# Last attention step and tail of the FFN in another order: probability copy before the maxima, gate chunks before the other batches' steps, down products before z, and z in two banks

## The chip, the cores and the metric

One Trainium2 chip, one core of it. The time is the device time in microseconds of one execution; the median of three runs is compared. Engines are named PE (TensorE), DVE (VectorE), ACT (ScalarE), POOL (GpSimd) and SP (SyncE, which issues the loads).

## The reference

Four layers over x of 8 batches x 128 tokens x 512, each added to its input after a layer norm without weights:

```python
x = x + cross_attention(layernorm(x), ctx, mask, bias, ...)   # 32 heads of 128, softmax over 128 keys
x = x + ffn(layernorm(x), w_gate, w_up, w_down)               # int8 fake quantisation, silu(gate) * up, 1376 wide
x = x + channel_attention(layernorm(x), ctx, conv_w, ...)     # top 76 of 128 of ctx per column, max/mean, conv, batch norm
x = x + routed_lora(layernorm(x), router_w, A, Bm)            # 8 experts, best 2
```

The third layer splits z = layernorm(x), transposed, by a mask of the context's largest values into two parts, takes the maximum and the mean of each over the tokens, sends both through a small convolution, and normalises over all batches: every batch's maxima and sums must be there before the convolution can start.

## The kernel before, in words

Each engine has one instruction stream, written out by hand; semaphores (`s_...`) are the only order between the engines, and an engine that waits holds all that stands behind it. Batches 0 to 3 go through 32 attention steps (one per head) first, then batches 4 to 7 through steps 32 to 63, in which the FFN and the z part of batches 0 to 3 are hidden (`turn(n, r)`). What is left behind step 63 is the tail: batches 4 to 7 (called k = 0 to 3 there) go through the FFN and the z part with nothing to hide them.

In step 63 PE makes scores in `pS`, DVE adds bias and mask, takes maxima, ACT takes exponentials, DVE multiplies by the inverse row sums (`prob`), PE transposes `prob` into `pS`, DVE copies it to `pT_sb` (L1402), PE makes `pT` from it and the values (L1983), ACT and DVE split that into `aT_hi` and `aT_lo` (L1351), and PE adds the output projection to `oacc` (L1731 to L1733, four batches, `outputs`). DVE also looks for the largest context values in every step (`pick_round`, MAX8 and MATCH_REPLACE, L1194 to L1200), and writes the found mask to `top` (L1413) in each fourth. `e_zshift` (L1396) is a shift for ACT's `z_again`.

In the tail, in this order for each k: `residual_of(k)` (L1454) adds `oacc` to `xr`; `token_stats` and POOL's `token_rstd` give the norm; `token_steps` (L1471 to L1480) the quantised tokens; PE transposes them, ACT writes `t_yqT` (`tokens_out`); PE's `gate_products` and `up_products` (L2043) fill `pA` in three chunks of 512, 512 and 352 columns; DVE's `gate_rows(k, j)` (L1489) empties a gate chunk, and only then PE may write the up chunk of the same columns; ACT's `gated_silu` and `up_out` and POOL's `up_rows` follow; `hidden(k)` (DVE, L1496 to L1506) multiplies and quantises; `hidden_transposes`, ACT's `hidden_out` (L976), `down_products` (PE into `pD`, L2078), `down_rows` (DVE, L1514); then `xr` takes the sum (`add_down` on POOL, or DVE in `z_stats`). For z: `z_stats(k)`, POOL's `z_rstd(k)`, DVE's `z_shift(k)` and ACT's `z_normal(k)` (or `z_here(k)`, all on DVE), PE's `z_transposes(k)`, then the split into `split` (ACT `z_out` and POOL `branches`, or DVE `branches_here`), DVE's `maxima(k)` (L1448) and ACT's `sums(k)` (L935). `pTb`, `pA`, `pD`, `pZ`, `pYb` are PSUM tensors that lie where the attention's `oacc`, `pX0`, `pX1`, `pS` and `pT` were; `s_x1_done` guards that. `z_transposes` had one bank, `pZ`.

Of the kernel before, what the change touches and what calls it, by code (L numbers as in the profile page):

```python
# [52 lines left out]
def layers_kernel(nc, x, cT, mask, bias, ln_w, wq, wk, wv, wo, w_gate, w_up, w_down,  # L53
# [12 lines left out]
    with ctx:  # L66
# [1033 lines left out]
        def _(dve):  # L1100
# [251 lines left out]

            def step(n, half, q, j, rows=False):
# [37 lines left out]
                if isinstance(n, int) and n == STEPS - 1:  # L1391
                    dve.wait_ge(s_e_zrs, HB)
                    dve.wait_ge(s_e_z_trans, HB - 1)
                    v.tensor_scalar(e_down[:], xr[:, HB - 1, :], e_zmv[:, HB - 1, 0:1], e_zrs[:, HB - 1:HB],
                                    ALU.subtract, ALU.mult).then_inc(s_e_z_t, 1)
                    v.scalar_tensor_tensor(out=e_zshift[:], in0=e_zmv[:, :, 0], scalar=-1.0, in1=e_zrs[:],  # L1396
                                           op0=ALU.mult, op1=ALU.mult).then_inc(s_e_zshift, 1)
# [7 lines left out]
                if j < 3:  # L1405
                    pick_round()
                else:
                    dve.drain()
                    for r in range(2):
                        tile = bass.ds(half * KT * NH + (2 * q + r) * S, S)  # L1410
                        if isinstance(q, int):
                            tile = slice(half * KT * NH + (2 * q + r) * S, half * KT * NH + (2 * q + r + 1) * S)
                        v.tensor_scalar(top_flat[:, tile], pick[:, r, ::-1], LOWEST, None, ALU.not_equal)  # L1413
# [311 lines left out]
        def _(pe):  # L1725
# [356 lines left out]
            def z_transposes(k):  # L2082
                if k < 2:
                    pe.wait_ge(s_z_act, k + 1)
                else:
                    pe.wait_ge(s_z_dve, k - 1)
                if k in (1, 2):
                    pe.wait_ge(s_zT, k)
                if k == 3:
                    pe.wait_ge(s_split_dve, 2)  # L2090
# [178 lines left out]
```

## Time and profile before

| | us |
|---|---|
| three runs | 1065.75, 1065.99, 1067.38 |
| median | 1065.99 |
| the profiled execution, its own time | 1069.71 |
| its span in the trace | 1068.0 |
| end of the last attention step's output products, start of the convolution | 946.4, 1013.6 |

The span runs from the first to the last instruction. The profiled execution's own time is 1.7 us above its span and 3.7 us above the median of the runs. All that the change touches lies between 933 us and 1014 us of the span.

### The profile page before, as it was taken

Reading aid. Unit: us, or ns where it says so; the run is one execution under the profiler, and the core shown is the slowest. Engines: PE = TensorE matmul, PEld = TensorE weight load, DVE = VectorE, ACT = ScalarE, POOL = GpSimd, SP = SyncE. Lnnn points to the kernel's source line nnn. Section 1 sums busy time; section 2 is a strip of 40 time slices with the busy share of each in tenths; the row PEclk is TensorE's granted clock in tenths of the full one; section 3 lists DMA queues with packets and bytes.
Section 4 is the critical chain, followed back from the end, with each engine's and each line's share of the span. In section 5 each row is a group of like instructions: output and inputs, shape, how many; then the busy total and the mean of one; then the engine's idle time right before and its main releaser. Section 6 shows DMA issues by size and latency. Waiting matters only on the chain.

```text
span 1068.0 us, 18238 instructions
## 1 busy us (share of the span) xinstructions
PE 996.8 (93%) x6004; PEld 843.0 (79%) x6004; DVE 697.6 (65%) x1827; ACT 512.6 (48%) x1328; POOL 467.5 (44%) x366
## 2 busy tenths in 40 slices
PE   5999999999999999999999999999999999869376
PEld 4888888888888888888888888888888888734263
DVE  5567565666577767677564575566567557678755
ACT  4454444444444445445543544445355354345561
POOL 4555444444444555443354344346435334226241
PEclk9999999999999999999999999999999999969768
DMA  6422222223333332333322222213222221000002
GB/s 219 161 92 87 95 95 89 91 95 96 96 97 98 98 97 83 104 112 98 106 84 84 85 67 72 83 42 98 73 74 84 80 69 53 23 21 1 0 2 79
DMA packets 50412, 87.71 MB, mean 82 GB/s; under 512 B 6368, under 2 KB 15200, under 8 KB 50336
## 3 DMA queue, kind: packets, MB, share of 16 engines
q1 hardware_dynamic: 50336, 86.76, 25.4%
q8 instruction: 40, 0.66, 0.2%
q14 instruction: 36, 0.29, 0.1%
HBM read 84.64 MB, written 2.10 MB: 81 GB/s over the span
## 4 chain that ended last, share of the span: by engine, by line
PE 79%; DVE 7%; issue 6%; POOL 3%; DVEq 2%; ACT 2%; DMA 1%; SPq 0%; POOLq 0%; ACTq 0%
PE pX L1731 15%; PE pX L1733 14%; PE pX L1732 14%; PE pT L1983 5%; PE oacc L1731 5%; PE oacc L1732 5%; PE oacc L1733 5%; PE pS L1915 5%; PE pS L1736 2%; PE pA L2043 1%; POOL wv_lo L570 1%; PE pX L1848 1%; PE pX L1904 1%; PE pT L1904 1%; PE pX L1736 1%
## 5 line engine op out<-in xcount | busy, mean ns | idle before, releaser
L570 POOL TENSOR_TENSOR wq_lo<-raw_q,wq_hi 128x512 fp32r<-128x512 f32 x64 | 82.6, 1290 | 264.2 <-DVE prob L1376 257.9
L1731 PE MATMUL pX<-wv_lo,cT_hi 128*128 128x256 f32 x512 | 149.5, 292 | 0.2 <-ACT q_sb L740 0.2
L1359 DVE TENSOR_TENSOR score<-pS,b_mask 128x512 f32<-128x512 f32 x64 | 44.2, 691 | 156.8 <-PE pS L1915 144.7
L868 ACT ACTIVATE prob<-score,neg_max 128x128 f32<-128x128 f32 x256 | 99.8, 391 | 97.4 <-DVE neg_max L1362 97.4
L1732 PE MATMUL pX<-wv_hi,cT_lo 128*128 128x256 f32 x512 | 144.3, 282 | 0.0
L1733 PE MATMUL pX<-wv_hi,cT_hi 128*128 128x256 f32 x512 | 144.2, 282 | 0.0
L570 POOL TENSOR_TENSOR wv_lo<-raw_v,wv_hi 128x1024 fp32r<-128x1024 f32 x32 | 77.1, 2409 | 121.9 <-ACT wv_hi L740 121.9
L740 ACT ACTIVATE v_sb<-pX 128x512 f32<-128x512 f32 x64 | 38.2, 597 | 163.6 <-PE pX L1733 163.6
L1731 PE MATMUL pX<-xT_lo,wq_hi 128*128 128x512 f32 x252 | 104.4, 414 | 5.7 <-POOL wq_lo L570 5.0
L1731 PE MATMUL oacc<-wo_lo,aT_hi 128*128 128x512 f32 x256 | 101.8, 398 | 3.5 <-DVE aT_lo L1351 2.3
L1731 PE MATMUL pX<-cT_lo,wk_hi 128*128 128x512 f32 x252 | 103.0, 409 | 0.0
L1732 PE MATMUL oacc<-wo_hi,aT_lo 128*128 128x512 f32 x256 | 101.0, 395 | 0.0
L1733 PE MATMUL oacc<-wo_hi,aT_hi 128*128 128x512 f32 x256 | 100.8, 394 | 0.0
L1733 PE MATMUL pX<-cT_hi,wk_hi 128*128 128x512 f32 x252 | 99.3, 394 | 0.0
L1732 PE MATMUL pX<-xT_hi,wq_lo 128*128 128x512 f32 x252 | 98.8, 392 | 0.0
L1732 PE MATMUL pX<-cT_hi,wk_lo 128*128 128x512 f32 x252 | 98.7, 392 | 0.0
L1733 PE MATMUL pX<-xT_hi,wq_hi 128*128 128x512 f32 x252 | 98.6, 391 | 0.0
L1732 PEld LDWEIGHTS pX<-wv_hi,cT_lo 128*128 128x128 f32 x512 | 98.0, 191 | 0.0
L1731 PEld LDWEIGHTS pX<-wv_lo,cT_hi 128*128 128x128 f32 x512 | 97.0, 190 | 0.5 <-ACT q_sb L740 0.5
L1733 PEld LDWEIGHTS pX<-wv_hi,cT_hi 128*128 128x128 f32 x512 | 97.0, 189 | 0.0
L740 ACT ACTIVATE wk_hi<-raw_k 128x512 fp32r<-128x512 f32 x64 | 40.4, 632 | 113.7 <-PE pX L1733 104.5
L570 POOL TENSOR_TENSOR wk_lo<-raw_k,wk_hi 128x512 fp32r<-128x512 f32 x64 | 83.0, 1298 | 26.7 <-ACT wk_hi L740 21.4
(308 smaller groups left out, 2377.4 us busy)
## 6 DMA issues: line engine op xcount, KB each, us to landing
raw_k<-in_wk SPq DMA_DIRECT2D x64, 256.0 KB, 2.8
raw_q<-in_wq SPq DMA_DIRECT2D x64, 256.0 KB, 3.5
raw_v<-in_wv SPq DMA_DIRECT2D x32, 512.0 KB, 3.9
raw_o<-in_wo SPq DMA_DIRECT2D x64, 256.0 KB, 2.6
b_raw<-in_bias SPq DMA_DIRECT2D x64, 64.0 KB, 2.5
g_raw<-in_w_gate SPq DMA_DIRECT2D x16, 172.0 KB
g_raw<-in_w_up SPq DMA_DIRECT2D x16, 172.0 KB
f_raw<-in_w_down SPq DMA_DIRECT2D x4, 688.0 KB, 4.1
```

The lines of the kernel that those rows point to most:

```text
L570: g.tensor_tensor(w_lo[c][:], w_raw[c][:], w_hi[c][:].bitcast(F32), ALU.subtract).then_inc(s_w_lo[c], 1)
L740: return a.activation(dst, src, ACT.Copy)
L868: e = a.activation(prob[:, b, :], score[:, b, :], ACT.Exp, bias=neg_max[:, b:b + 1], accum_out=row_sum[:, b:b + 1])
L1359: v.tensor_tensor(score[:], pS[:].rearrange("p (b s) -> p b s", b=HB), b_mask[:], ALU.add).then_inc(s_scored, 1)
L1731: mm(dst, lh, rl, start=start, stop=False, skip_group_check=lint)
L1732: mm(dst, ll, rh, start=False, stop=False, skip_group_check=lint)
L1733: return mm(dst, lh, rh, start=False, stop=stop, skip_group_check=lint)
L1736: return mm(dst, src, ident, is_transpose=True, start=True, stop=True)
L1848: last = mm(pX0[:], e_hqT[0:deep, k * S:(k + 1) * S], wdT[0:deep, k, :], start=k == 0, stop=k == IT - 1)
L1904: last = mm(bank[:, 0:c1 - c0], y_qT[:, kt * S:(kt + 1) * S], w_rowT[up_half][:, kt, c0:c1], start=kt == 0, stop=kt == KT - 1)
L1915: last = mm(pS[:, cols], q_sb[:, cols], k_sb[:, cols], start=True, stop=True)
L1983: last = mm(pT[:, cols], v_sb[parity][:, b, heads], pT_sb[:, cols], start=True, stop=True)
```

## The change

No arithmetic is added or removed; instructions are put in another order, one takes another bank, one addition goes from DVE to POOL, and one batch's z from DVE to ACT.

- Last step: the copy to `pT_sb` comes ahead of `e_zshift` and of the last `pick_round`; the write of `top` (`picked`) goes behind the first `token_stats`, where `largest(e_split, 3)` was. That one goes behind `token_steps(1, 2)`.
- `gate_rows(0, 0)` to `gate_rows(0, 2)` come ahead of the waits on other batches' norms. `gate_products(0)` may start when three `residual_of` are done, not four; batches 2 and 3 wait for the fourth.
- `hidden(3)` comes ahead of `z_shift(0)`; PE's `hidden_transposes(3)` ahead of `z_transposes(0)`, and `down_products(3)` ahead of `z_transposes(1)`. `z_transposes` uses `pZ` and `pYb` in turn.
- k = 2: POOL adds (`add_down(2)`) and ACT normalises (`z_normal(2)`), ahead of `sums(0)`.

```diff
+        z_bank = (pZ, pYb[:].bitcast(F32))
...
-            sp.wait_ge(s_x1_done, 2)
+            sp.wait_ge(s_x1_done, 3)
...
             add_down(1)
+            z_rstd(1)
+            add_down(2)
             branches(0)
-            z_rstd(1)
             z_rstd(2)
...
             z_normal(0)
+            hidden_out(3)
             z_out(0)
-            hidden_out(3)
             z_normal(1)
+            z_out(1)
+            z_normal(2)
             sums(0)
-            z_out(1)
...
-                pick_round(last=j == 3)
+                if not end:
+                    pick_round(last=j == 3)
                 if unless_last(n + 1):
                     key_out(n + 1)
                 dve.wait_ge(s_p_trans, n + 1)
                 v.tensor_copy(pT_sb[:], pS[:]).then_inc(s_pT, 1)
...
+                if end:
+                    v.scalar_tensor_tensor(out=e_zshift[:], in0=e_zmv[:, :, 0], scalar=-1.0, in1=e_zrs[:],
+                                           op0=ALU.mult, op1=ALU.mult).then_inc(s_e_zshift, 1)
+                    pick_round(last=True)
...
             token_stats(0, 1)
-            largest(e_split, HB - 1).then_inc(s_maxed, 1)
+            picked(1, H // 4 - 1)
             residual_of(1)
...
-            residual_of(2)
+            residual_of(2).then_inc(s_x1_done, 1)
             residual_of(3).then_inc(s_x1_done, 1)
             token_stats(1, HB)
-            v.memset(prb[:, :, E:2 * E], LOWEST)
+            gate_rows(0, 0)
             dve.wait_ge(s_y_rstd, 2)
...
-            gate_rows(0, 0)
+            gate_rows(0, 1)
+            gate_rows(0, 2)
             dve.wait_ge(s_y_normal, 1)
             token_steps(1, 2)
-            gate_rows(0, 1)
-            gate_rows(0, 2)
+            largest(e_split, HB - 1).then_inc(s_maxed, 1)
+            v.memset(prb[:, :, E:2 * E], LOWEST)
...
             down_rows(1)
+            hidden(3)
             z_shift(0)
-            hidden(3)
             z_stats(1)
             down_rows(2)
+            z_shift(1)
             z_stats(2)
-            z_shift(1)
             maxima(0)
-            z_here(2)
+            z_shift(2)
             down_rows(3)
             z_stats(3)
             branches_here(2)
+            maxima(1)
             z_here(3)
-            maxima(1)
+            maxima(2)
             branches_here(3)
-            maxima(2)
             maxima(3)
...
             token_transposes(1)
             gate_products(1)
+            pe.wait_ge(s_x1_done, 3)
             token_transposes(2)
...
             down_products(2)
+            hidden_transposes(3)
             z_transposes(0)
-            hidden_transposes(3)
+            down_products(3)
             z_transposes(1)
-            down_products(3)
             z_transposes(2)
```

The order on DVE at the end of the last attention step, before. `e_down` here is the z of batch 3; MAX and MATCH_REPLACE are the pick round.

```order
L1394 TENSOR_SCALAR e_down<-xr,e_zmv,e_zrs 128x512 [waits early_z_trans,early_zrs]
L1396 SCALAR_TENSOR_TENSOR e_zshift<-e_zmv,e_zrs 128x4
L1194 MAX pick<-pick 128x8 x2
L1197 MEMSET pick 128x2x4
L1200 MATCH_REPLACE pick<-pick 128x128 x2
L1402 COPY pT_sb<-pS 128x512 [waits p_trans]
L1413 TENSOR_SCALAR top<-pick 128x128 x2
L1351 TENSOR_TENSOR aT_lo<-pT,aT_hi 128x512 [waits a_hi]
```

The same place of the change:

```order
L1394 TENSOR_SCALAR e_down<-xr,e_zmv,e_zrs 128x512 [waits early_z_trans,early_zrs]
L1413 COPY pT_sb<-pS 128x512 [waits p_trans]
L1417 SCALAR_TENSOR_TENSOR e_zshift<-e_zmv,e_zrs 128x4
L1197 MAX pick<-pick 128x8 x2
L1200 MEMSET pick 128x2x4
L1203 MATCH_REPLACE pick<-pick 128x128 x2
L1354 TENSOR_TENSOR aT_lo<-pT,aT_hi 128x512 [waits a_hi]
```

The copy to `pT_sb` now stands right behind `e_down`, and the write of `top` is gone from between it and `aT_lo`.

DVE again, from the statistics of batches 1 to 3 of the tail to the steps of batches 2 and 3, before (`t_y` are the tokens, `e_gate<-pA` the gate chunks of k = 0):

```order
L1463 BN_AGGR t_ymv<-t_yst 128x2 x3
L1465 TENSOR_SCALAR t_yve<-t_ymv 128x3
L1570 MEMSET prb 128x8x8
L1572 SCALAR_TENSOR_TENSOR t_yshift<-t_ymv,t_yrs 128x3 [waits y_rstd]
L1489 SCALAR_TENSOR_TENSOR e_gate<-pA,y_steps,g_row 128x512 [waits g_proj]
L1471 TENSOR_REDUCE t_ymax<-t_y 128x1 [waits y_normal]
L1474 TENSOR_SCALAR y_steps<-t_ymax 128x1
L1477 RECIPROCAL t_yinv<-y_steps 128x1
L1480 TENSOR_SCALAR t_y<-t_y,t_yinv 128x512
L1489 SCALAR_TENSOR_TENSOR e_gate<-pA,y_steps,g_row 128x512 [waits g_proj]
L1489 SCALAR_TENSOR_TENSOR e_gate<-pA,y_steps,g_row 128x352 [waits g_proj]
L1471 TENSOR_REDUCE t_ymax<-t_y 128x2 [waits y_normal]
```

And in the change:

```order
L1475 TENSOR_SCALAR t_yve<-t_ymv 128x3
L1499 SCALAR_TENSOR_TENSOR e_gate<-pA,y_steps,g_row 128x512 [waits g_proj]
L1582 SCALAR_TENSOR_TENSOR t_yshift<-t_ymv,t_yrs 128x3 [waits y_rstd]
L1499 SCALAR_TENSOR_TENSOR e_gate<-pA,y_steps,g_row 128x512 [waits g_proj]
L1499 SCALAR_TENSOR_TENSOR e_gate<-pA,y_steps,g_row 128x352 [waits g_proj]
L1481 TENSOR_REDUCE t_ymax<-t_y 128x1 [waits y_normal]
L1484 TENSOR_SCALAR y_steps<-t_ymax 128x1
L1487 RECIPROCAL t_yinv<-y_steps 128x1
L1490 TENSOR_SCALAR t_y<-t_y,t_yinv 128x512
L1458 TENSOR_REDUCE stat<-e_split 128x4 x2
L1589 MEMSET prb 128x8x8
L1481 TENSOR_REDUCE t_ymax<-t_y 128x2 [waits y_normal]
```

All three gate chunks now stand ahead of the steps of batch 1, the first of them ahead of the wait for `y_rstd` too, and the maxima of `e_split` stand behind those steps.

PE at the end of the FFN, from the transposes of `hidden(2)` on, before (`h_mag` is what `hidden` leaves, `e_hqT` what `hidden_out` leaves):

```order
L1736 MATMUL pTb<-ident_b,h_mag 96x128
L2078 MATMUL pD<-wdT,e_hqT 128x512 [waits d_used,h_qT]
L2078 MATMUL pD<-wdT,e_hqT 128x512 x10
L1736 MATMUL pZ<-ident,z 128x128 [waits z_by_act]
L1736 MATMUL pZ<-ident,z 128x128 x3
L1736 MATMUL pTb<-ident_b,h_mag 128x128 [waits h_qT,h_mag]
L1736 MATMUL pTb<-ident_b,h_mag 128x128 x9
L1736 MATMUL pTb<-ident_b,h_mag 96x128
L1736 MATMUL pZ<-ident,z 128x128 [waits zT,z_by_act]
L1736 MATMUL pZ<-ident,z 128x128 x3
L2078 MATMUL pD<-wdT,e_hqT 128x512 [waits d_used,h_qT]
L2078 MATMUL pD<-wdT,e_hqT 128x512 x10
```

And in the change:

```order
L1747 MATMUL pTb<-ident_b,h_mag 96x128
L2089 MATMUL pD<-wdT,e_hqT 128x512 [waits d_used,h_qT]
L2089 MATMUL pD<-wdT,e_hqT 128x512 x10
L1747 MATMUL pTb<-ident_b,h_mag 128x128 [waits h_qT,h_mag]
L1747 MATMUL pTb<-ident_b,h_mag 128x128 x9
L1747 MATMUL pTb<-ident_b,h_mag 96x128
L1747 MATMUL pZ<-ident,z 128x128 [waits z_by_act]
L1747 MATMUL pZ<-ident,z 128x128 x3
L2089 MATMUL pD<-wdT,e_hqT 128x512 [waits d_used,h_qT]
L2089 MATMUL pD<-wdT,e_hqT 128x512 x10
L1747 MATMUL pYb<-ident,z 128x128 [waits z_by_act]
L1747 MATMUL pYb<-ident,z 128x128 x3
```

The transposes of `hidden(3)` and the last down products each stand one group earlier, z's first group stands between them, and its second goes to `pYb` behind the down products.

## Rows read from the trace of the kernel before

**Rows 1.** The page: the chain that ended last, shares of the span by engine.
```profile
PE 79%; DVE 7%; issue 6%; POOL 3%; DVEq 2%; ACT 2%; DMA 1%; SPq 0%; POOLq 0%; ACTq 0%
```

**Rows 2.** Timeline of DVE: start, duration, instruction, [idle before <- releaser].
```profile
934.05 1.23 DVE L1396 SCALAR_TENSOR_TENSOR e_zshift<-e_zmv,e_zrs 128x4 f32<-128x4 f32 x1
...
936.64 0.68 DVE L1402 COPY pT_sb<-pS 128x512 f32<-128x512 f32 x1
...
940.12 0.69 DVE L1351 TENSOR_TENSOR aT_lo<-pT,aT_hi 128x512 fp32r<-128x512 f32 x1 [2.34 <-ACT aT_hi L740]
...
942.55 0.69 DVE L1454 TENSOR_TENSOR xr<-oacc,xr 128x512 f32<-128x512 f32 x1 [0.17 <-PE oacc L1733]
...
944.42 1.27 DVE L1448 TENSOR_REDUCE stat<-e_split 128x4 f32<-128x512 f32 x2
```

**Rows 3.** Timeline of PE, same columns, steps 62 and 63 and the first products.
```profile
926.82 1.16 PE L1983 MATMUL pT<-pT_sb,v_sb 128*128 128x128 f32 x8 [0.94 <-DVE pT_sb L1402]
...
933.74 0.66 PE L1736 MATMUL pS<-ident,prob 128*128 128x128 f32 x4 [1.22 <-DVE prob L1376]
...
937.38 2.08 PE L1983 MATMUL pT<-pT_sb,v_sb 128*128 128x128 f32 x8 [2.52 <-DVE pT_sb L1402]
...
949.79 4.13 PE L2043 MATMUL pA<-wgT,t_yqT 128*128 128x512 bf16 x12 [0.80 <-DVE xr L1454]
...
956.86 2.66 PE L2043 MATMUL pA<-wuT,t_yqT 128*128 128x512 bf16 x8 [1.63 <-DVE e_gate L1489]
...
960.65 4.20 PE L2043 MATMUL pA<-wgT,t_yqT 128*128 128x512 bf16 x12 [0.71 <-ACT t_yqT L953]
```

**Rows 4.** Windows: stretch, length, busy us of PE, PEld, DVE, ACT, POOL, PEclk, DMA.
```profile
936.84:947.08 10.24, 7.57 (x20) 5.59 (x20) 7.15 (x15) 5.22 (x20) 0.55 (x1) 0.50 0.00 1
...
957.31:964.14 6.83, 6.12 (x20) 2.54 (x19) 4.91 (x6) 2.97 (x4) 2.67 (x3) 0.50 0.00 0
...
965.40:979.80 14.40, 14.40 (x93) 8.08 (x92) 13.26 (x18) 8.96 (x14) 9.81 (x7) 1.00 0.00 1
```

**Rows 5.** Timeline of DVE, tokens and gate chunks of the tail.
```profile
954.42 0.69 DVE L1471 TENSOR_REDUCE t_ymax<-t_y 128x1 f32<-128x512 f32 x1 [0.29 <-ACT t_y L947]
...
956.06 1.23 DVE L1489 SCALAR_TENSOR_TENSOR e_gate<-pA,y_steps,g_row 128x512 f32<-128x512 f32 x2
957.38 1.22 DVE L1471 TENSOR_REDUCE t_ymax<-t_y 128x2 f32<-128x1024 f32 x1
...
959.16 2.60 DVE L1480 TENSOR_SCALAR t_y<-t_y,t_yinv 128x512 f32<-128x512 f32 x2
...
965.44 1.58 DVE L1496 TENSOR_TENSOR silu<-silu,e_up 128x1376 f32<-128x1376 f32 x1
```

**Rows 6.** Timeline of POOL around `z_rstd(0)` and `add_down(1)`.
```profile
986.54 0.54 POOL L695 TENSOR_TENSOR t_zrs<-t_zve,neg_half 128x1 f32<-128x1 f32 x1
987.05 1.26 POOL L690 TENSOR_TENSOR xr<-xr,e_down 128x512 f32<-128x512 f32 x1
```

**Rows 7.** Timeline of DVE, end of the FFN.
```profile
987.11 1.22 DVE L1534 SCALAR_TENSOR_TENSOR t_zshift<-t_zmv,t_zrs 128x1 f32<-128x1 f32 x1 [0.76 <-POOL t_zrs L695]
988.25 1.58 DVE L1496 TENSOR_TENSOR silu<-silu,up 128x1376 f32<-128x1376 f32 x1
...
1003.17 0.75 DVE L1514 SCALAR_TENSOR_TENSOR e_down<-pD,h_steps,sd_row 128x512 f32<-128x512 f32 x1 [3.81 <-PE pD L2078]
```

**Rows 8.** Tile `h_mag`, DVE: duration ns min/median/max, first and last start us.
```profile
L1506 DVE TENSOR_SCALAR h_mag<-silu,h_s x4: 936/942/1770, 969.2 to 992.1; 128x1376 f32<-128x1376 f32 x4
```

**Rows 9.** Timeline of PE, last down products, z and convolution.
```profile
999.53 3.61 PE L2078 MATMUL pD<-wdT,e_hqT 128*128 128x512 bf16 x11
...
1013.63 0.66 PE L2132 MATMUL pA<-stat,band 128*128 128x64 f32 x2 [4.88 <-DVE stat L1448]
```

**Rows 10.** Timeline of ACT: the copy behind the last hidden transposes.
```profile
994.71 1.24 ACT L976 ACTIVATE e_hqT<-pTb 128x1280 bf16<-128x1280 int16 x1 [4.18 <-PE pTb L1736]
```

**Rows 11.** Groups of ACT, 998.6 to 1012.6: the four batches' sums, | busy, mean ns | idle.
```profile
L935 ACT ACTIVATE zc<-split 128x128 f32<-128x128 f32 x32 | 9.4, 295 | 3.6 <-POOL split L702 2.6 <-DVE split L1442 0.8
```

More of the change, by code:

```diff
@@ L990, in z_out @@
                     act.wait_ge(s_sf, k)
-                copy(zT[:], pZ[:].rearrange("p (k s) -> p k s", k=KT)).then_inc(s_zT, 1)
+                copy(zT[:], z_bank[k][:].rearrange("p (k s) -> p k s", k=KT)).then_inc(s_zT, 1)
             def sums(k):
@@ L1351, in attended_low, with picked @@
                 v.tensor_tensor(aT_lo[:], pT[:], aT_hi[:].bitcast(F32), ALU.subtract).then_inc(s_a_lo, 1)
+            def picked(half, q):
+                dve.drain()
+                for r in range(2):
+                    tile = bass.ds(half * KT * NH + (2 * q + r) * S, S)
+                    if isinstance(q, int):
+                        tile = slice(half * KT * NH + (2 * q + r) * S, half * KT * NH + (2 * q + r + 1) * S)
+                    v.tensor_scalar(top_flat[:, tile], pick[:, r, ::-1], LOWEST, None, ALU.not_equal)
             def step(n, half, q, j, rows=False):
@@ L1378, in step @@
                 early_first_bank(n)
+                if end:
+                    dve.wait_ge(s_e_zrs, HB)
+                    dve.wait_ge(s_e_z_trans, HB - 1)
+                    v.tensor_scalar(e_down[:], xr[:, HB - 1, :], e_zmv[:, HB - 1, 0:1], e_zrs[:, HB - 1:HB],
+                                    ALU.subtract, ALU.mult).then_inc(s_e_z_t, 1)
                 if second_x(n) is not None:
@@ L1390, in step @@
                                                op0=ALU.mult, op1=ALU.subtract)
[L1391 to L1397, printed above, removed]
-                pick_round(last=j == 3)
+                if not end:
+                    pick_round(last=j == 3)
                 if unless_last(n + 1):
@@ L1404, in step @@
                     residual(0)
-                if j < 3:
+                if end:
+                    v.scalar_tensor_tensor(out=e_zshift[:], in0=e_zmv[:, :, 0], scalar=-1.0, in1=e_zrs[:],
+                                           op0=ALU.mult, op1=ALU.mult).then_inc(s_e_zshift, 1)
+                    pick_round(last=True)
+                elif j < 3:
                     pick_round()
                 else:
[L1408 to L1413, printed above, removed]
+                    picked(half, q)
                 early_end(n)
@@ L1517, in z_stats @@
             def z_stats(k):
-                if k < 2:
+                if k < 3:
                     dve.wait_ge(s_d_added, k + 1)
@@ L1546, in branches_here @@
                 dve.wait_ge(s_summed, HB + k - 1)
-                masked(split[k % 2], pZ, 1, k, s_split_dve)
+                masked(split[k % 2], z_bank[k % 2], 1, k, s_split_dve)
             def maxima(k):
@@ L1642, in _ @@
             dve.wait_ge(s_e_z_again, HB)
-            dve.wait_ge(s_z_act, 2)
+            dve.wait_ge(s_z_act, 3)
             def gated(t):
@@ L2082, in z_transposes @@
             def z_transposes(k):
-                if k < 2:
+                if k < 3:
                     pe.wait_ge(s_z_act, k + 1)
                 else:
[L2086 to L2090, printed above, removed]
+                    pe.wait_ge(s_z_dve, 1)
+                if k >= 2:
+                    pe.wait_ge(s_zT, k - 1)
                 for kt in range(KT):
-                    last = tr(pZ[:, kt * S:(kt + 1) * S], z[:, HB + k, kt * P:(kt + 1) * P], ident[:])
+                    last = tr(z_bank[k % 2][:, kt * S:(kt + 1) * S], z[:, HB + k, kt * P:(kt + 1) * P], ident[:])
                 last.then_inc(s_z_trans, 1)
```

2 lines of the change are left out of this document (1 added, 1 removed).

## Prediction

> **What bounds the kernel now.** First the chain that ended last: PE holds 79% of it [rows 1], but that is the attention steps, which the change leaves alone. So the timeline of each engine was read from step 63 to the convolution. There PE waits. In step 63 it stands idle for 2.52 us until DVE has copied the transposed probabilities [rows 3], although their transposes end at 933.74 + 0.66 = 934.40 and the copy starts at 936.64 [rows 2, 3]: on DVE `e_zshift` and the pick round stand in between. Then the windows: the granted clock of PE is 0.50, its lower level of 1.2 GHz, from 936.84 to 947.08 and again from 957.31 to 964.14, each time after such idle stretches [rows 4]. In the first products of the tail PE waits 1.63 us for gate chunks that DVE empties late [rows 3]. From 965.4 to 979.8 PE is busy 14.40 us of 14.40 and DVE 13.26 [rows 4]: no order helps there, what is won ahead of it is kept at best. Behind it DVE, POOL and ACT pass one batch after another from hand to hand, and the convolution waits for the last maxima, PE idle for 4.88 us [rows 9].
>
> So there are three places to price: step 63, the first products, and the end from the third `down_rows` on.
>
> **Step 63.** The copy can start when the transposes are done, 934.4 instead of 936.64: 2.2 us. `e_zshift` and the pick round go behind it. `e_zshift` took 1.23 us at 934.05 [rows 2], ending at 935.28; with POOL as it is it ends at about that time wherever it starts, so the round ends as before, at 936.7. Next late would be `aT_lo`, which stood at 940.12 [rows 2]. The `pT` products took 2.08 us at the lower clock and 1.16 us one step earlier, at the higher [rows 3]. With only 0.4 us of idle ahead of them I take the higher clock, another 0.9 us, so `aT_lo` is wanted at 940.12 - 3.1 = 937.0. The round is thus hidden by 0.3 us; were it not, its lateness would come off the gain one for one. `residual_of(0)` waited for PE 0.17 us only [rows 2], so it follows DVE's chain and comes at 939.4 instead of 942.55.
>
> Bounds of the clock: at the lower one the gain there is 2.2 us and not 3.1. I take the higher, since its row is the one with a gap of 0.94 us, the nearer one [rows 3].
>
> **First products.** Between `residual_of(0)` and the tokens of batch 0 stood `largest`, 1.27 us from 944.42 [rows 2]. In its place comes the write of `top`, two 128x128 operations and a drain; no row of mine holds them, but they are a quarter of the width of the 0.69 us copy each [rows 2], so I take 0.4 us together (bounds 0.2 and 0.8). That gives 0.9 us more: `gate_products(0)` starts at about 945.8 instead of 949.79 [rows 3]. That three residuals are enough saves little, because the tokens' path (norm, steps, transposes, copy by ACT) ends at the same time as the fourth residual; I count nothing. The constants' loads wait for the fourth residual as before, since the count they wait for rises with it.
>
> PE then has been idle for some 5 us, so I give `gate_products(0)` the lower clock: 1376 columns x 4 / 1.2 GHz = 4.6 us, to 950.4. It took 4.13 us before, partly at each [rows 3]. Meanwhile DVE does the statistics of batches 1 to 3 and two of the chunks. From 950.4 DVE is the path: the last chunk (0.6 us, half of the 1.23 us for two [rows 5]); the steps of batch 1 (956.06 - 954.42 = 1.65 us [rows 5]); `largest`, now here, 1.3; the steps of batches 2 and 3 (959.16 - 957.38 = 1.8 us, then the last operation twice); the three chunks of batch 1, 1.9 (1.23 for two and the wait-free third). The last operation twice took 2.60 us [rows 5], its POOL neighbour `up_rows(0)` running at the same time; in the new order POOL is done with that, and I take 1.1, half of the steps' remaining time; 2.60 is the upper bound. Sum: 950.4 + 0.6 + 1.7 + 1.3 + 1.8 + 1.1 + 1.9 = 958.8. Before, `hidden(0)` started at 965.44 [rows 5]. PE keeps up: `up_products(0)` needs no chunk that is late, the 1.63 us wait is gone, and `gate_products(1)` starts near 954.2 instead of 960.65, under the time it has until DVE wants it, even at its old 4.20 us (958.4, 0.5 us late at most). So the gain at `hidden(0)` is **6.6 us**, of which 3.1 are from step 63, 0.9 from `largest`, 2.6 from the chunks. Through the full stretch up to 979.8 it is carried, no more and no less.
>
> **End of the FFN**, in the old times, as if nothing had been won ahead. `hidden(3)` stood behind `z_shift(0)`, which waited 0.76 us for POOL and then took 1.22 us where the work is one column: it started at 987.11, while POOL's `add_down(1)` ran from 987.05 for 1.26 us, and both ended at 988.3 [rows 6, 7]. Now `hidden(3)` needs only `up_rows(3)`, which POOL ends right ahead of `z_rstd(0)` at 986.54 [rows 6]. It reads two tiles of SBUF, as `z_shift` does, and so may have to let `z_rstd(0)` end first, at 987.1 (0.5 us), which I take. It started at 988.25 [rows 7] with POOL's end at 988.31. In the old order its last operation was the longest of four, 1.77 us where the median is 0.94 [rows 8], beside POOL's split of batch 0; another 0.8 us goes, as POOL's split is later now. `h_mag` is ready at 991.6 instead of 993.8: 2.2 us.
>
> The Trainium skill (SBUF — State Buffer, Who interferes with whom) says that a DVE operation with two SBUF inputs and a GpSimd operation that reads SBUF exclude each other for a whole instruction. The trace agrees (1.22 us for one column, above). By that rule `hidden(3)` loses the 0.5 us; by its own row alone (1.58 us, unhindered) the sum would be 0.5 us better.
>
> PE transposes `h_mag` (0.8), z of batch 0 (0.6), and ACT's copy takes 1.24 us and a short second one [rows 10]: the down products can start at 994.0. They took 3.61 us, between the clocks [rows 9]; bounds 2.4 and 4.7 us (11 x 512 columns at 2.4 and 1.2 GHz). They end between 996.4 and 998.7, not at 1003.1. But DVE gets to `down_rows(3)` only behind `maxima(0)`, and that waits for POOL: `down_rows(2)` ends near 993.7, `add_down(2)` 1.26 later, the split of batch 0 two operations of like length, so 997.5; the maxima take 1.3 (as in [rows 2]) and `down_rows(3)` starts at **998.9** instead of 1003.17 [rows 7], 4.3 us earlier, at either clock.
>
> From there to the convolution it was 1013.63 - 1003.17 = 10.46 us [rows 7, 9]. Now ACT does `z_normal(2)` ahead of `sums(0)`, and `branches_here(2)` waits for `sums(0)`. One batch's sums take (9.4 + 6.0) / 4 less the overlap; the 32 pairs fill 9.4 us, so 2.4 us [rows 11]. `z_normal(2)` can start at 999.0 to 1000.3, so `sums(0)` ends at 1002.3 to 1003.5. Then DVE: the split 1.5, `maxima(1)` 1.3, `z_here(3)` 0.5, `maxima(2)` 1.3, the split 1.5, `maxima(3)` 1.3, to 1009.7 to 1010.9. The convolution starts 2.8 to 3.9 us earlier: **3.3 us**. About 1 us of the 4.3 is thus given back in the wait for `sums(0)`.
>
> **Sum.** 6.6 + 3.3 = 9.9 us, off the profiled execution's own 1069.71: 1059.8. The median of the runs is 3.7 us below that own time. I take 0.6 us of gain off, because the lower clock from 957.31 to 964.14 [rows 4] is part of the 15.7 us that the trace shows between `gate_products(0)` and `hidden(0)`, and a faster execution may have less of it. 1065.99 - 9.3 = 1056.7.
>
> **The rivals.**
> *The clock does not come.* PE stays at 1.2 GHz in step 63 (gain 2.2, not 3.1), the output products then take their lower-clock time, and the median's executions of before had a better clock in `gate_products(1)` than this trace, up to 1.7 us (half of 4.20, less the rest). The gain is then 9.9 - 0.9 - 0.5 - 1.7 = 6.8, at worst, with the end at 2.8, 6.3 us: 1059.2 to 1059.7. For it: the clock was 0.50 for 10 us there. Against: the gap ahead of `pT` shrinks from 2.52 to 0.4 us. Chance 0.18.
> *The end gives it all back.* Each us by which `sums(0)` is later is a us at the convolution; if POOL's two additions, split and DVE's short operations exclude each other in turn, two waits of 1.2 us and one of 0.6 stand in that chain and the 3.3 us are gone: 1066.0 - 6.0 = 1060.0. For it: the 1.22 us row. Against: ACT still needs only 9.6 us for the four sums. Chance 0.08.
> *It does nothing that can be measured.* The path does not run where I read it, and step 63 and the first products are hidden by PE's 14.40 us. Against: PE waits for DVE in front of each. 1066, chance 0.02.
> *Slower.* The clock stays at 1.2 GHz through the stretch in which PE is busy for all of its 14.40 us. It would then need 28.8 us, a loss of 14.4, and the result is 1066 - 9.9 + 14.4 = 1070.5. The break-even is at 9.9 / 14.4 = 0.69 of the stretch, and slower by over 0.2% needs 0.83 of it. For it: PE enters the stretch with less done ahead of it. Against: the stretch had clock 1.00 here, and so had each in which PE had worked without a gap. Chance 0.02.
>
> **How the numbers follow.** My forecast has 0.70, with its own range 1054.3 to 1058.7: down by 2.4 for the unhindered bounds (`hidden(3)` 0.5, the end at 3.9, a `gate_products(0)` at the higher clock, the top write at its lower bound), up by 2 for the opposite. To leave out no more than 2 in 10 the range takes in the clock's rival and most of the end's: 1054.3 to 1060.0. 0.2% (2.1 us) is about what a measurement of this kernel can tell from no change. Faster 0.95, same 0.03, slower 0.02.
>
> **What would show it.** Right: the copy to `pT_sb` within 0.2 us of the transposes' end, `pT` in 1.2 us, `residual_of(0)` 3 us earlier, no wait of PE for gate chunks, `hidden(0)` 6 to 7 us earlier, the stretch behind it as long as before, `hidden(3)` ahead of `z_shift(0)` with a last operation of 0.94 us, and DVE waiting for `sums(0)`, where it did not. Wrong: a pick round that ends behind `aT_hi`; a lower clock between 933 and 941; DVE idle between the chunks; `down_rows(3)` less than 4 us earlier; a change of length ahead of 933 or behind the convolution of over 1 us.

## The result, and the profile after

| | before | changed | |
|---|---|---|---|
| median of the runs | 1066.49 us (1065.75 to 1067.38, 4 runs) | 1060.06 us (1059.44 to 1061.64, 4 runs) | ratio 0.994, 95% interval 0.9924 to 0.9956 |
| profiled execution, own time | 1069.71 us | 1059.44 us | 10.3 less |
| its span | 1068.0 us | 1057.7 us | 10.3 less |

The kernel is 6.4 us faster; 9.3 us were forecast, and 1060.06 lies just outside the range, which ended at 1060.0. Yet the two profiled executions differ by 10.3 us. The first difference is one of medians, the second one of two single executions; the gap between them is what this study is about.

DVE in step 63 and in the tokens, timeline of the changed kernel (start, duration, instruction, [idle before <- releaser]); the answers to [rows 2] and [rows 5]:

```profile
934.32 0.69 DVE L1413 COPY pT_sb<-pS 128x512 f32<-128x512 f32 x1 [0.29 <-PE pS L1747]
934.93 0.24 DVE L1417 SCALAR_TENSOR_TENSOR e_zshift<-e_zmv,e_zrs 128x4 f32<-128x4 f32 x1
...
936.89 0.69 DVE L1354 TENSOR_TENSOR aT_lo<-pT,aT_hi 128x512 fp32r<-128x512 f32 x1 [0.28 <-ACT aT_hi L742]
...
939.06 0.68 DVE L1464 TENSOR_TENSOR xr<-oacc,xr 128x512 f32<-128x512 f32 x1
...
941.09 0.38 DVE L1363 TENSOR_SCALAR top<-pick 128x128 bf16<-128x128 f32 x2
...
952.59 1.13 DVE L1490 TENSOR_SCALAR t_y<-t_y,t_yinv 128x512 f32<-128x512 f32 x1
...
956.84 0.88 DVE L1490 TENSOR_SCALAR t_y<-t_y,t_yinv 128x512 f32<-128x512 f32 x2
...
959.45 1.58 DVE L1506 TENSOR_TENSOR silu<-silu,e_up 128x1376 f32<-128x1376 f32 x1
```

The copy starts 0.04 us behind the last transpose (933.62 + 0.66 = 934.28), the pick round is over when `aT_hi` comes (DVE idle for 0.28 us), and `hidden(0)` starts at 959.45 instead of 965.44.

PE in the same stretch and at the end of the FFN, for [rows 3] and [rows 9]:

```profile
935.07 1.16 PE L1994 MATMUL pT<-pT_sb,v_sb 128*128 128x128 f32 x8 [0.33 <-DVE pT_sb L1413]
...
946.15 4.11 PE L2054 MATMUL pA<-wgT,t_yqT 128*128 128x512 bf16 x11 [1.16 <-ACT t_yqT L955]
...
954.86 2.50 PE L2054 MATMUL pA<-wgT,t_yqT 128*128 128x512 bf16 x12 [0.69 <-ACT t_yqT L955]
...
987.41 2.55 PE L2089 MATMUL pD<-wdT,e_hqT 128*128 128x512 bf16 x10 [0.71 <-ACT e_hqT L979]
...
1003.79 0.66 PE L2142 MATMUL pA<-stat,band 128*128 128x64 f32 x2 [3.28 <-DVE stat L1458]
```

`pT` has the higher clock; `gate_products(0)` still has the lower one for most of its time; `gate_products(1)` takes 2.50 us where it took 4.20 in [rows 3]; the last down products 2.55 where they took 3.61 in [rows 9]. The convolution starts 9.84 us earlier.

DVE at the end of the FFN, for [rows 7] and [rows 8]:

```profile
980.32 1.59 DVE L1506 TENSOR_TENSOR silu<-silu,up 128x1376 f32<-128x1376 f32 x1 [0.33 <-POOL up L685]
...
984.14 0.94 DVE L1516 TENSOR_SCALAR h_mag<-silu,h_s 128x1376 f32<-128x1376 f32 x1
984.99 0.15 DVE L1544 SCALAR_TENSOR_TENSOR t_zshift<-t_zmv,t_zrs 128x1 f32<-128x1 f32 x1
...
992.60 0.74 DVE L1524 SCALAR_TENSOR_TENSOR e_down<-pD,h_steps,sd_row 128x512 f32<-128x512 f32 x1
...
996.22 0.69 DVE L1452 TENSOR_TENSOR split<-pZ,top 128x512 f32<-128x512 f32 x1 [0.41 <-ACT zc L937]
```

`hidden(3)` goes first, `z_shift(0)` takes 0.15 us instead of 1.22, the last `h_mag` 0.94 instead of 1.77, `down_rows(3)` starts at 992.60 instead of 1003.17, and DVE waits 0.41 us for `sums(0)`.

### The profile page after: what moved, and what is told of

Its sections match the earlier page's. It is cut to its first block, busy times and chain, and to the rows that moved or that the text cites. A ratio compares the mean times of both kernels' runs of the same rounds, so it can differ in the third digit from the quotient of the medians.

```text
span 1057.7 us, 18220 instructions
## 1 busy us (share of the span) xinstructions
PE 990.2 (94%) x5987; PEld 838.8 (79%) x6004; DVE 693.1 (66%) x1826; ACT 513.0 (49%) x1329; POOL 471.5 (45%) x367
## 4 chain that ended last, share of the span: by engine, by line
PE 78%; DVE 6%; issue 6%; POOL 4%; ACT 2%; DVEq 2%; DMA 1%; SPq 0%; ACTq 0%; POOLq 0%
PE pX L1742 15%; PE pX L1744 15%; PE pX L1743 15%; PE pT L1994 5%; PE oacc L1742 5%; PE oacc L1743 5%; PE oacc L1744 5%; PE pS L1926 5%; PE pS L1747 2%; POOL wv_lo L571 1%; PE pT L1915 1%; PE pX L1859 1%; PE pX L1915 1%; POOL up L685 1%; DMA raw_k<-in_wk 1%
```

## The experiments

All times are medians in us. Ratios are to runs of the kernel before on the same chip, taken together with them, with 95% intervals. The experiments come in four sets; each has its own runs of before.

### Set 1: the parts one by one (before 1066.87, 32 runs)

**p1_same**, the kernel before without an edit.

> The kernel before, unchanged. Theory K (the clock): the profiled execution of before (own time 1069.7, 3.2 us above the median 1066.5) was slow because PE's granted clock fell to 1.2 GHz in an unlucky place of the tail. Then another execution of the same program has an own time between 1065 and 1068, its first 933 us alike within 0.3 us, and the missing 2 to 4 us between 933 us and the end, where the windows show the lower clock in other stretches. Theory P (profiling): an execution that is profiled is always some 3 us slower; then this one's own time is 1069 or more again, with the same stretches.

1066.94 (12 runs), ratio 0.9998 [0.9987, 1.0009]. Its profiled execution took 1066.94 us, the median itself. So the profile that the prediction worked from, with 1069.71, was of a long execution: the 32 runs of before in this set spread from 1064.3 to 1070.8, and only two of them were longer. Being profiled does not by itself cost the 3 us (theory P); theory K's signs came, with step 63 starting at 933.58 against 933.74 and the difference behind it.

**p2_copy_first**, the copy ahead of `e_zshift` and the pick round.

```diff
-                    v.scalar_tensor_tensor(out=e_zshift[:], ...)
-                pick_round(last=j == 3)
+                if not end:
+                    pick_round(last=j == 3)
...
                 v.tensor_copy(pT_sb[:], pS[:]).then_inc(s_pT, 1)
+                if end:
+                    v.scalar_tensor_tensor(out=e_zshift[:], ...)
+                    pick_round(last=True)
```

> The first part alone: in the last attention step the copy to pT_sb ahead of e_zshift and the pick round. By the sum of the prediction 3.1 us (2.2 of earlier copy, 0.9 of clock), less 0.2 because the write of top still stands ahead of aT_lo. Theory K: the parts' gains measured as medians add to about 6.4 us, and this one is worth 2 to 3. Rival: it is worth the whole 3.1 and another part is worth next to nothing.

1063.22 (12 runs), 0.9965 [0.9954, 0.9977]: 3.7 us, 1.2 us either way; it can't tell K's 2 to 3 from 3.1.

**p3_gates_first**, the chunks of batch 0 ahead of `token_steps(1, 2)`, with `largest` and the memset behind it.

```diff
-            largest(e_split, HB - 1).then_inc(s_maxed, 1)
             residual_of(1)
...
             token_stats(1, HB)
-            v.memset(prb[:, :, E:2 * E], LOWEST)
+            gate_rows(0, 0)
             dve.wait_ge(s_y_rstd, 2)
...
-            gate_rows(0, 0)
-            dve.wait_ge(s_y_normal, 1)
-            token_steps(1, 2)
             gate_rows(0, 1)
             gate_rows(0, 2)
+            dve.wait_ge(s_y_normal, 1)
+            token_steps(1, 2)
+            largest(e_split, HB - 1).then_inc(s_maxed, 1)
+            v.memset(prb[:, :, E:2 * E], LOWEST)
```

> The second part alone: gate_rows(0, 0..2) ahead of the steps of batch 1, and the maxima of e_split behind them. By the sum of the prediction 0.9 + 0.4 (no top write in its place) + 2.6 = 3.9 us. Theory K: the part of the 2.6 us that came from the low clock in gate_products(1) of before's trace (up to 1.7) is not there at the median, so 2 to 2.5 us. Rival: 3.9 us in full.

1066.29 (12 runs), 0.9989 [0.9977, 1.0002]: 0.6 us, less than can be told from nothing, and less than either theory had said.

**p4_end_only**, the end part alone: `hidden(3)` first, the down products ahead of z, z in two banks, z of batch 2 by ACT and its addition by POOL.

> The third part alone: hidden(3) ahead of z_shift(0), the down products ahead of z, two banks, batch 2's z on ACT. By the sum of the prediction 3.3 us. The trace of the change shows 33.8 us from hidden(2) to the convolution before and 30.3 after, 3.5 us. Theory K: 3 to 3.5 us here too, since the clock played no part in it. Rival (the end gives it back at the median): under 1.5 us.

1062.60 (9 runs), 0.9963 [0.9949, 0.9977]: 4.3 us. The three parts sum to 8.6 us, the whole gives 6.4. With some 1.3 us either way on each part that is no proof that together they are worth less than apart.

### Set 2: without the gate part, and PE filled in the first products (before 1066.96, 15 runs)

**q1_after**, the changed kernel again.

> The changed kernel, unchanged, with as many runs as the parts had. The parts measured 3.7 (copy), 1.2 or less (gates) and 3.9 us (end); if they add, 8.5 us and a ratio near 0.992. If the four runs so far (0.994, 6.4 us) stand, the parts overlap by 2 us.

1060.43 (5 runs), 0.9939 [0.9926, 0.9953].

**q2_copy_end**, the edits of p2 and p4 together: the change without its gate part. The write of `top` and the fourth `residual_of` also stand where they were before.

> The change without its second part (the gate chunks and the maxima of e_split stay where they were before). Theory K: with the copy ahead and the clock up, the gate part is worth under 1 us at the median, so this kernel is within 1 us of the change. Rival (the prediction's 2.6 us for the chunks and 0.5 for the maxima): it is 3 us slower than the change.

1058.76 (5 runs), 0.9918 [0.9904, 0.9931]: 1.7 us under the whole change, whose gate part so looked like a loss (the two intervals just touch). The 3 us that the prediction's terms gave for this part are excluded.

**q3_before_filled** and **q4_after_filled**: 26 and 28 matmuls whose results are never read, in PE's gaps from 934 to 961 us, as in

```diff
+            filler(pZ, 14)
             token_transposes(0)
+            filler(pZ, 4)
```

> The kernel before with 26 matmuls of 512 columns (results never read) on PE in its idle stretches from 934 to 961 us, so that it does not stand still; each batch of them is shorter than the gap that it fills. Theory K: the granted clock stays at 1.00 from 933 to 965, the stretch from gate_products(0) to hidden(0) takes 13.0 us or less instead of 13.8 to 15.7, the times are 2 to 3 us lower and closer together. Rival (the clock follows something else, or does not set these stretches): no faster, or slower by the matmuls that do not fit.

> The changed kernel with 28 such matmuls in its gaps from 936 to 955 us. Theory K: clock 1.00 through them, gate_products(0) takes 2.5 us instead of 4.1, but DVE is the path there, so the gain is 0.3 to 1 us only, and the change keeps 5 to 6 us over the filled kernel before. This would be the fastest kernel so far. Rival: nothing or slower.

q3 1065.88 (11 runs), 0.9986 [0.9977, 0.9996]; q4 1059.71 (5 runs), 0.9926 [0.9912, 0.9939]. By the medians these matmuls are worth 1.1 us to before and 0.7 us to the change, and the difference stays at 6.2 us. The traces say more of before: the stretch to `hidden(0)` fell from 30.09 us in p1_same to 28.15 in q3 (25.83 to 25.37 in the change), but q3's execution had reached step 63 late, at 935.06 instead of 933.58, ahead of the first of these matmuls; no run says why.

### Set 3: PE filled behind the FFN (before 1066.67, 14 runs)

Matmuls that nobody reads, here of 128 columns on the identity, in six places from the last z transposes to the last `hidden_transpose`, in before, in the change and in the edits of q2; the fourth kernel moves only `largest` in q2's.

```diff
+            filler(16)
             z_transposes(3)
+            filler(10)
...
             lora(3)
+            filler(22)
             hidden_transpose(4)
```

> The kernel before with matmuls of no use (their results are overwritten) in five idle gaps of PE from the last z transposes to the last `hidden_transpose`. Theory A, that the granted clock behind the convolution differs from kernel to kernel and takes part of the gain: the low clock from just behind the convolution on (24 us in a copy of before) goes or shortens, the stretch from the first `coef` to the end falls from 44.3 to 46.1 us to under 44, the time is 1.5 to 3 us under before. Theory B, that the clock there is worth little because DVE and ACT set the pace: within 0.5 us of before, or up to 1 us slower by matmuls that stand in the way.

> The same matmuls in the changed kernel. Theory A: its low clock there is the longer one (27 us), so it gains more than before does, 2.5 to 4 us: about 1057, 8 to 9 us under the filled before, which is the gain that the trace shows up to the convolution. Theory B: 1060.4 as without them, 6.5 us under the filled before.

> The same matmuls in the version without the gate part. Theory A: 1.7 us of difference between it and the change came from the clock, so the two filled versions stand within 0.5 us of each other, at about 1057. Theory C, that the gate part loses its time by its own order on DVE: it stays 1.5 to 2 us under the filled change.

> The version without the gate part, with `largest` moved behind `token_steps(1, 2)` and the gate chunks where they were: half of the gate part. Theory A (the clock behind the convolution decides, by where a kernel's gaps fall): its time goes with the length of the low stretch there, 1058.8 with 24 us of it, 1060.4 with 27 us. Theory C: 1058.8 if the chunks' order costs the time, 1060.4 if the place of `largest` does.

r1 1063.27 (9 runs), 0.9971 [0.9961, 0.9981]; r2 **1055.15** (4 runs), 0.9894 [0.9879, 0.9908]; r3 **1054.41** (5 runs), 0.9888 [0.9873, 0.9902]; r4 1060.46 (6 runs), 0.9947 [0.9934, 0.9959]. By matmuls that compute nothing the change gains 5.0 us (11.5 us under before of its set instead of 6.5 in set 2), before 3.4 us, and the 1.7 us between q1 and q2 shrink to 0.7. Theory A has the direction of r1, r2 and r3 right, with more gained than it said (3.4 us for 1.5 to 3, 5.0 for 2.5 to 4). It fails on r4: behind the convolution r4 took 53.2 us, no longer than q2 with 53.3, and it lost its time ahead of it. r2 and r3, with s3 and s4 below, are the fastest kernels here, 5 to 6 us under the change.

Windows of r2 behind its convolution (stretch, length, busy us of PE, PEld, DVE, ACT, POOL, PEclk, DMA):

```profile
1003.80:1012.06 8.26, 7.94 (x41) 7.65 (x42) 3.21 (x15) 2.70 (x8) 0.71 (x1) 0.59 0.01 2
1012.06:1043.80 31.74, 26.01 (x181) 20.77 (x181) 20.51 (x76) 18.24 (x50) 14.27 (x16) 1.00 0.09 34
1043.80:1053.40 9.60, 6.05 (x28) 3.23 (x27) 4.07 (x11) 1.00 (x4) 0.00 (x0) 0.97 0.29 110
```

The same windows without the matmuls, in the changed kernel (it ends at 1057.7 and not at 1053.4, though both convolutions start at 1003.8):

```profile
1003.79:1012.05 8.26, 3.94 (x16) 3.61 (x16) 2.10 (x12) 1.55 (x5) 0.70 (x1) 0.50 0.00 0
1012.05:1023.79 11.74, 9.35 (x46) 7.95 (x47) 6.78 (x17) 8.76 (x23) 5.83 (x6) 0.60 0.00 1
1023.79:1043.79 20.00, 15.58 (x96) 11.15 (x95) 12.66 (x46) 10.57 (x30) 8.44 (x11) 1.00 0.11 40
1043.79:1057.70 13.91, 6.58 (x12) 2.47 (x12) 6.34 (x28) 1.27 (x5) 0.00 (x0) 0.75 0.25 95
```

and in p1_same, whose convolution starts at 1012.62:

```profile
1012.62:1020.88 8.26, 3.94 (x16) 3.61 (x16) 2.10 (x11) 1.37 (x3) 0.70 (x1) 0.50 0.01 2
1020.88:1032.62 11.74, 9.07 (x49) 7.43 (x49) 6.91 (x18) 9.42 (x24) 6.61 (x7) 0.66 0.00 1
1032.62:1052.62 20.00, 15.06 (x92) 10.88 (x92) 13.16 (x47) 9.93 (x28) 7.66 (x9) 1.00 0.11 40
1052.62:1065.20 12.58, 6.13 (x12) 2.39 (x12) 5.74 (x26) 1.27 (x5) 0.00 (x0) 0.86 0.28 105
```

The work behind the convolution is the same in both kernels. The changed one has clock 0.60 against 0.66 in the second window and 0.75 against 0.86 in the last, and needs 53.91 us against 52.58: 1.3 us of what was won is lost there. Other traces of the same orders without matmuls in this part spread as well: before 54.37 and 52.45 (q3), the change 54.3 (q1) and 54.2 (q4). The last window holds the plainest rows. PE in it, changed kernel:

```profile
1047.71 0.69 PE L1747 MATMUL pA<-ident,hw 128*128 128x128 f32 x2 [4.12 <-DVE hw L1702]
1048.55 2.07 PE L2196 MATMUL pYb<-lb,hwT 128*128 128x512 f32 x2 [0.15 <-ACT hwT L742]
```

and in r2, with the gap filled:

```profile
1045.40 0.38 PE L1747 MATMUL pA<-ident,hw 128*128 128x128 f32 x2
1046.04 1.12 PE L2204 MATMUL pYb<-lb,hwT 128*128 128x512 f32 x2 [0.26 <-ACT hwT L742]
```

After 4.12 us of idle the same product takes 2.07 us, at a granted clock of 0.50 (1.2 GHz), and with the gap filled 1.12 us, at 1.00 (2.4 GHz). That activity releases PE's clock and idleness halves it is what the Trainium skill says (TensorE: Matmul & The Clock Gate, Part 1); these rows agree.

### Set 4: PE filled from 934 us to the end (before 1066.45, 9 runs)

Both sets of matmuls, with one or two gaps more at the end of the FFN, in four kernels, so that the clock nearly drops out of their differences: the mean granted clock of the traces is 0.995 to 1.000. The number of matmuls is fitted to each kernel's gaps.

> The kernel before with matmuls of no use in the gaps of step 63 and of the first products too, and in four gaps of the end of the FFN: PE's granted clock at its higher level nearly throughout from 934 us to the end. It is the yardstick for the three others. Both theories: 1061 to 1062.5 (the two sets of such matmuls alone gave 1.3 and 3.6 us).

> The gate part alone (chunks ahead of other batches' steps, `largest` and the memset later) with the same matmuls. Theory D (the prediction's term of 3.5 us for this part was right and the clock hid it): 3 us or more under the filled before. Theory E (in the trace of before 1.8 us of that stretch was a lower clock in `gate_products(1)`, and the order alone is worth little): 0.3 to 1.5 us under it.

> The change without the gate part, with the same matmuls. Theory A (the order of the gate part costs nothing by itself, its loss comes from the clock behind the convolution): 0 to 1.5 us above the filled change. Theory C: 1.5 us or more under it.

> The whole change with the same matmuls. Theory A: 8 to 9.5 us under the filled before, near the 9.3 of the prediction, at about 1053 to 1054. Theory B (the gain really is 6.4 us by the order of the work): 6.5 us under it.

s1 1060.56 (5 runs), 0.9946 [0.9933, 0.996]; s2 1058.58 (5 runs), 0.9927 [0.9913, 0.994]; s3 1055.67 (4 runs), 0.9899 [0.9884, 0.9914]; s4 1055.02 (4 runs), 0.989 [0.9874, 0.9905]. The kernel before gains 5.9 us by the matmuls alone, nearly what the whole change brings. The whole change is worth 5.5 us against s1: theory A's 8 to 9.5 us is refuted, and with it the view that the clock had only hidden a gain of 9; theory B's 6.5 is within the uncertainty. Of the gate part alone D expected 3 us or more and E at most 1.5: 2.0 us measured (s1 to s2) is neither; in the change it gives 0.7 us (s3 to s4), as theory A said and theory C did not. Each of these two is uncertain by some 1.5 us either way, and the second includes the write of `top`. The traces of s1 and s2 differ by 1.1 us from the transposes of `prob` to `hidden(0)`, and by 0.5 us to the end; another 1.2 us of their difference lies ahead of step 63, which no edit touches. So E's size is the one that the traces bear out.

Windows of s1, from the transposes of `prob` in step 63 to `hidden(0)`, to `hidden(3)`, to the convolution, to the end:

```profile
934.47:962.62 28.15, 21.66 (x112) 11.62 (x113) 23.66 (x54) 14.30 (x34) 6.53 (x6) 0.94 0.08 21
962.62:985.08 22.46, 20.23 (x127) 10.75 (x126) 20.37 (x28) 13.61 (x20) 18.74 (x13) 1.00 0.00 1
985.08:1009.13 24.05, 19.30 (x156) 16.39 (x155) 19.99 (x35) 13.89 (x70) 6.90 (x8) 1.00 0.00 1
1009.13:1058.50 49.37, 39.45 (x252) 31.05 (x252) 27.89 (x101) 21.76 (x58) 14.97 (x17) 0.96 0.12 43
```

the same of s4:

```profile
935.45:960.82 25.37, 21.68 (x119) 11.70 (x120) 21.98 (x54) 14.92 (x35) 6.60 (x6) 1.00 0.09 23
960.82:981.70 20.88, 18.32 (x114) 9.52 (x112) 19.12 (x28) 12.80 (x19) 18.11 (x12) 1.00 0.00 1
981.70:1005.17 23.47, 19.81 (x137) 14.77 (x138) 19.05 (x34) 14.54 (x72) 10.40 (x10) 0.93 0.00 1
1005.17:1054.20 49.03, 38.02 (x252) 29.44 (x252) 27.88 (x101) 21.93 (x60) 14.97 (x17) 1.00 0.12 44
```

and, not filled, of p1_same:

```profile
933.58:963.67 30.09, 20.33 (x82) 11.93 (x84) 23.56 (x53) 14.16 (x33) 6.81 (x6) 0.72 0.07 19
963.67:986.48 22.81, 20.42 (x127) 11.10 (x129) 20.43 (x29) 13.96 (x21) 18.08 (x13) 1.00 0.00 1
986.48:1012.62 26.14, 9.60 (x44) 5.46 (x43) 19.83 (x35) 13.89 (x70) 6.55 (x8) 0.66 0.00 0
```

The granted clock was not full everywhere: it is 0.94 and 0.96 in the first and the last stretch of s1, and 0.93 in the third of s4, where the down products of batch 2 took 4.24 us, as they did in the changed kernel. That cost nothing there: the stretch is 23.47 us in both.

## Why the prediction missed

The table takes the same four stretches from five executions, us. The columns of before and of the change are worked out from the starts in [rows 3, 5, 7, 9], from the spans and from the rows of after above.

| stretch | before | p1_same | changed | before less changed | p1_same less changed | s1 less s4 (gaps filled) |
|---|---|---|---|---|---|---|
| `prob` transposes to `hidden(0)` | 31.70 | 30.09 | 25.83 | 5.9 | 4.3 | 2.8 |
| to `hidden(3)` | 22.81 | 22.81 | 20.87 | 1.9 | 1.9 | 1.6 |
| to the convolution | 25.38 | 26.14 | 23.47 | 1.9 | 2.7 | 0.6 |
| to the end | 54.37 | 52.58 | 53.91 | 0.5 | -1.3 | 0.3 |
| sum | 134.26 | 131.62 | 124.08 | 10.2 | 7.5 | 5.3 |

The spans of s1 and s4 differ by 4.3 us only, since in s4's execution the transposes of `prob` began 1.0 us later (935.45 against 934.47). Over all traces here that start lies between 931.7 and 935.5, ahead of every edit; why is not known, and it is one reason why a gain is read by stretches.

- **The order of the work was foreseen.** The sum was 9.9 us at the convolution; it started 9.84 us earlier in the profiled executions. That it fits so well is partly luck: `hidden(0)` came 6.0 us earlier and not 6.6, and from there on 3.85 us were won and not 3.3. Copy, pick round, `aT_lo`, the order of `hidden(3)`, the last `h_mag` and the wait for `sums(0)` came where the prediction put them.
- **The step that failed** is the last of the sum: "1065.99 - 9.3 = 1056.7". Terms read in one execution, one 3.7 us above the median, were taken off the median with 0.6 us of allowance. The median execution did not hold what some of these terms removed. p1_same shows it: 30.09 us for the first stretch instead of 31.70. From `gate_products(0)` to `hidden(0)` alone it took 13.8 us at a mean clock of 0.75, where the trace of before had 15.7 us at 0.67.
- **The terms that were mis-sized** are "2.6 from the chunks" and "0.9 from `largest`", 3.5 us together. The part measured 0.6 us alone and 0.7 to 2.0 us with the gaps filled. These rows show where the 3.5 us stood, from before, from p1_same (two rows) and from p2, whose only edit is the copy:

```profile
964.28 1.24 DVE L1489 SCALAR_TENSOR_TENSOR e_gate<-pA,y_steps,g_row 128x512 f32<-128x512 f32 x2 [0.95 <-PE pA L2043]
```

```profile
960.57 2.50 PE L2043 MATMUL pA<-wgT,t_yqT 128*128 128x512 bf16 x12 [0.71 <-ACT t_yqT L953]
...
961.85 1.90 DVE L1489 SCALAR_TENSOR_TENSOR e_gate<-pA,y_steps,g_row 128x512 f32<-128x512 f32 x3 [0.95 <-ACT silu L969]
```

```profile
957.58 1.89 DVE L1492 SCALAR_TENSOR_TENSOR e_gate<-pA,y_steps,g_row 128x512 f32<-128x512 f32 x3
```

  In before DVE waited for `gate_products(1)`, which took 4.20 us [rows 3]. In p1_same these products took 2.50 us, and DVE waited for ACT. The 2.6 us were therefore mostly the lower clock of one execution; the prediction named up to 1.7 us for this and kept it for a rival. In p2, with the old order of the gate chunks, DVE had no idle left ahead of them. So beside the copy the gate part had little to win, as the stretch to `hidden(0)` shows in every trace, us:

| | old order | gate part alone | copy, without the gate part | both |
|---|---|---|---|---|
| not filled here | 31.70 (before), 30.09 (p1_same), 29.32 (p4), 29.33 (r1) | 28.24 (p3) | 26.02 (p2), 26.64 (q2), 26.02 (r3) | 25.83 (changed), 26.16 (q1), 25.93 (r2) |
| filled | 28.15 (q3), 28.15 (s1) | 27.06 (s2) | 26.12 (s3) | 25.37 (q4), 25.37 (s4) |

  Where nothing is filled the copy takes some 3 to 4 us off p1_same, p4 and r1; the gate part takes 1.1 to 1.9 us off without the copy and 0 to 0.8 with it.
- **Behind the convolution nothing was to change.** There the change gives 1.3 us back against a typical execution of before, to a lower clock. The prediction had listed a change of over 1 us there as a sign of being wrong, but gave it no term and no rival.
- **Step 63 (3.1 us forecast):** 3.7 us measured alone. Right as far as it can be told, with the 0.9 us of clock: `pT` took 1.16 us, and `residual_of(0)` started 3.5 us earlier (939.06 instead of 942.55).
- **The end (3.3 us forecast):** 4.3 us alone. The prediction called its 4.3 us at `down_rows(3)` the same "at either clock". For the new order that holds: from `hidden(3)` to the convolution it took 22.9 to 23.5 us in all ten traces that have it, filled or not. The old order depends on the clock: 24.9 to 26.4 us in six traces, 24.0 in the two with all of it filled (s1, s2). With the gaps filled the two stretches from `hidden(0)` to the convolution are shorter by 2.2 us, not by 3.8 to 4.6: in before the low clock had lengthened the last down products, on the path. They took 3.61 us in [rows 9], 2.55 in the change, and in s1

```profile
995.96 2.54 PE L2088 MATMUL pD<-wdT,e_hqT 128*128 128x512 bf16 x11
```

- **`hidden(3)` beside `z_rstd(0)`:** 0.5 us was allowed for the exclusion of the two engines. It took 1.59 us and began at 980.32, while POOL was in that operation, so the allowance was not needed. The stretched one was POOL's next, `add_down(1)`:

```profile
980.18 0.54 POOL L696 TENSOR_TENSOR t_zrs<-t_zve,neg_half 128x1 f32<-128x1 f32 x1
980.70 2.34 POOL L691 TENSOR_TENSOR xr<-xr,e_down 128x512 f32<-128x512 f32 x1
```

  It took 1.26 us in [rows 6].
- **The rivals.** "The clock does not come" gave 1059.2 to 1059.7, near the result, for partly the right reason (up to 1.7 us of better clock in `gate_products(1)`), but its other half, no higher clock in `pT`, did not happen. "The end gives it all back", 1060.0, did not happen either.

In one line: of the 9.3 us forecast, 5.5 are the order of the work, measured by s1 and s4. The clock adds 0.9 us net to make the 6.4 measured: before loses about 5.9 us to the low clock (1066.45 against 1060.56), the changed kernel about 4.9 (6.5 us under before unfilled, 11.4 filled). Against p1_same the first stretch gave 2.3 us less than forecast, the end 1.3 us more, and the part behind the convolution took 1.3 us back.

What stays open: that the gate part costs 1.7 us in the unfilled change (q1 against q2) is explained by the clock only so far as the difference falls to 0.7 us with the last part filled (r2, r3) and turns to a gain of 0.7 us with all filled (s3, s4), all of it within the intervals. At the convolution the traces of q1 and q2 agree within 0.03 us; behind it they take 54.3 and 53.3. Why moving `largest` alone costs 2.0 us (r4 is 6.2 us under before of its set, q2 8.2) is settled for a part of it only. In r4 `largest` stands ahead of the second gate chunk, and PE waits for that:

```profile
953.47 3.06 PE L2049 MATMUL pA<-wuT,t_yqT 128*128 128x512 bf16 x8 [2.50 <-DVE e_gate L1495]
```

In q2 it waited 0.84 us and the eight products took 1.63. In r4's trace `hidden(0)` is 0.6 us later than in q2's, `down_rows(3)` 0.95 us; the rest is open.

## What to carry to other kernels

A tail in which PE waits a good part of the time has no single length: its clock follows the gaps, and a change of order moves the gaps. Before a term is taken from one trace, profile the unchanged kernel again and set the two traces side by side stretch by stretch; a term that only one of them shows is a guess about the median. When two terms shorten the same stretch, look for what each leaves for the other: beside the copy the chunks had next to nothing to win. To learn what an order is worth, fill PE's gaps with matmuls that nobody reads in both versions and compare those; and try such matmuls for their own sake, as they brought 5.0 us here on top of the change, nearly as much as the change itself.

## What the runs showed of the hardware

- The lower clock behind a gap was as expected; its size was not. 5.9 us of 1066 hung on it in a kernel whose mean granted clock reads 0.974 (p1_same).
- Two executions of one kernel (before and p1_same) differed by 1.8 us in the 15 us of the first products and by 1.8 us behind the convolution, with the same instructions in the same order. The granted clock was 0.67 against 0.75 in the former, and in the latter 0.76 over the last 14.4 us against 0.86 over the last 12.6.
- A one-input DVE operation is stretched too beside POOL: scaling a batch's tokens (L1490, 128x512) took 1.13 us in the changed kernel, beside POOL's `up_rows(0)`, and the next two together 0.88 us, with POOL idle. In s1 the last `h_mag` took 1.79 us beside POOL's split, in s4, without it, 0.94.
- A wait can fall on either side: where DVE's `hidden(3)` ran first, POOL's addition took 2.34 us instead of 1.26 (2.35 in s4).
